# Separate written orders for the edge iterations of a software-pipelined Mamba and MoE layer

## What is computed

```python
q = rope(x @ W_in[:256].T);  h = rmsnorm(q)                       # part p
z, xBC, dt = split(h @ W_zxbcdt.T)                                # part a
xBC = silu(conv4(xBC));  dt = softplus(dt + dt_bias)
y = ssd(x_ssm, dt, A, B, C)           # chunked scan over the sequence, with a carried state
x1 = x + layernorm(q + rmsnorm(y * silu(z)) @ W_out.T)
w, idx = route(sigmoid(f @ router.T)) # f = layernorm(x1); 2 of 4 groups, 4 of 16 experts   # part f
acc = shared_ffn(f) + sum_e w_e * ffn_e(f)                        # silu(f @ G) * (f @ U) @ Wd
out = x1 + layernorm(acc)                                         # part g
```

## Time and profile before

| | us |
|---|---|
| median of 3 runs | 3214.55 (3213.54 to 3217.93) |
| the profiled execution | 3218.34 |
| its span, first to last instruction | 3216.4 |
| PE busy | 3116.9 (97%) |
| DVE, POOL, ACT busy | 2393.1, 2033.7, 1931.1 |
| PE's share of the chain that ended last | 94% |
| mean granted clock of PE | 0.991 |

### The profile page before, as it was taken

One profiled execution on the slowest core, in us unless ns is written; L12 is line 12 of the kernel. 1 busy time (PEld: TensorE's weight loads), 2 busy tenths in 40 slices (PEclk: granted clock), 3 DMA queues, 4 the chain that ended last, 5 costly groups with the idle time before them and its releaser, 6 DMA issues.

```text
span 3216.4 us, 62379 instructions
## 1 busy us (share of the span) xinstructions
PE 3116.9 (97%) x19648; PEld 2723.4 (85%) x19648; DVE 2393.1 (74%) x5104; ACT 1931.1 (60%) x4146; POOL 2033.7 (63%) x2311
## 2 busy tenths in 40 slices
PE   3699999999999999999999999999999999999997
PEld 3588888888888888888888888888888888888886
DVE  3777777777777777777777777777777777777772
ACT  3566665566665566665666665666665656665652
POOL 0466666766666776666776666776666776666764
PEclk9799999999999999999999999999999999999999
DMA  3122222222222222222222222222222222222221
GB/s 109 40 70 80 66 59 74 73 76 79 66 60 75 72 77 78 66 60 74 72 78 76 66 63 72 72 79 76 66 65 71 71 79 76 66 67 69 71 80 40
DMA packets 143434, 227.33 MB, mean 71 GB/s; under 512 B 18977, under 2 KB 88353, under 8 KB 143393
## 3 DMA queue, kind: packets, MB, share of 16 engines
q1 hardware_dynamic: 126496, 210.06, 19.9%
q0 software_dynamic: 16896, 16.78, 4.0%
HBM read 174.87 MB, written 35.13 MB: 65 GB/s over the span
## 4 chain that ended last, share of the span: by engine, by line
PE 94%; POOL 1%; DMA 0%; DVE 0%; ACT 0%; issue 0%; SPq 0%; POOLq 0%; ACTq 0%; DVEq 0%
PE fpb L1325 33%; PE apb L1325 19%; PE acc L1504 17%; PE apb L1450 7%; PE apb L1334 4%; PE ppb L1325 3%; PE apb L1435 3%; PE apb L1442 2%; PE ppb L1344 2%; PE apb L1422 1%; PE fpb L1374 1%; PE fpb L1344 1%; PE fpb L1376 1%; PE fpb L1483 0%; PE apb L1395 0%; POOL hid L541 0%
## 5 line engine op out<-in xcount | busy, mean ns | idle before, releaser
L546 POOL TENSOR_TENSOR hidL<-hid,hidH 128x512 fp32r<-128x512 f32 x384 | 545.8, 1421 | 216.8 <-ACT hidH L801 207.5
L1015 DVE SCALAR_TENSOR_TENSOR xc<-apb,cw,xc 128x511 f32<-128x511 f32 (+2 forms) x576 | 427.8, 748 | 67.8 <-ACT xc L714 39.5
L1504 PE MATMUL acc<-WDH,hidH 128*128 128x256 f32 x1536 | 458.2, 298 | 6.2 <-POOLq L548 5.9
L801 ACT CAST hidH<-hid 128x512 fp32r<-128x512 f32 x384 | 236.1, 615 | 353.6 <-POOL hid L541 288.7
L1504 PE MATMUL acc<-WDH,hidL 128*128 128x256 f32 x1536 | 432.0, 281 | 0.0
L1504 PE MATMUL acc<-WDL,hidH 128*128 128x256 f32 x1536 | 431.5, 281 | 0.0
L541 POOL TENSOR_TENSOR hid<-hid,cb 128x512 f32<-128x512 f32 x256 | 347.2, 1356 | 81.8 <-DVEq L1136 43.7
L1134 DVE TENSOR_TENSOR hid<-hid,fpb 128x512 f32<-128x512 f32 x384 | 261.1, 680 | 135.4 <-PE fpb L1325 125.2
L1325 PE MATMUL fpb<-fTh,UH 128*128 128x512 f32 x768 | 336.1, 438 | 0.8 <-ACTq L793 0.8
L732 ACT ACTIVATE seg<-seg,acs 128x128 f32<-128x128 f32 x1024 | 313.8, 389 | 10.2 <-ACT cb L782 5.9
L1325 PE MATMUL fpb<-fTh,GH 128*128 128x512 f32 x768 | 317.5, 413 | 0.0
(11 more groups left out here) (194 smaller groups left out, 8672.1 us busy)
## 6 DMA issues: line engine op xcount, KB each, us to landing
seg<-acs_row SPq DMA_DIRECT2D x128, 512.0 KB, 4.2
cb<-c_row SPq DMA_DIRECT2D x512, 128.0 KB, 2.9
xsP<-in_x SPq DMA_DIRECT2D x32, 512.0 KB, 3.6
xc<-qrot SPq DMA_DIRECT2D x32, 512.0 KB, 3.4
xc<-in_x SPq DMA_DIRECT2D x32, 512.0 KB, 4.3
out<-xc SPq DMA_DIRECT2D x32, 512.0 KB, 3.0
out<-xn POOLq DMA_DIRECT2D x32, 512.0 KB, 6.0
ZL_loaded<-in_wzx_t SPq DMA_DIRECT2D x2, 512.0 KB, 5.7
```

Of the source, the lines that this page charges most:

```text
L546: own.do(G.tensor_tensor(hidL[:, j % 2, :], hid[:, j % 2, :], hidH[:, j % 2, :].bitcast(fp32), ALU.subtract))
L801: A.copy(hidH[:, j % 2, :], hid[:, j % 2, :]).then_inc(sem["hidden_high"], 1)
L1015: ins = V.scalar_tensor_tensor(xc[:, b, s:], src[:, 0:T - s], cw[:, b, TAPS - 1 - s:TAPS - s], xc[:, b, s:], ALU.mult, ALU.add)
L1504: ins = nc.tensor.matmul(dst, l[:, w, tk], r[:, j, :], start=j == 0 and t % 2 == 0 and n == 0, stop=j == HB - 1 and n == 2, skip_group_che ...
```

## The change

Each engine's `iteration` with flags is replaced by six functions written out, `lead`, `first`, `iteration`, `tail`, `drain`, `last`. `iteration`, used for the second iteration (without g) and for the loop, emits what it did before. The other orders are new on all engines, and each has its own bank tables (`PLANS`, looked up by a small class `Way`), so that results of a part can go round the banks in another sequence. Counts per iteration are the same. The splits have a semaphore each (`s_high[n]`, `s_low[n]`) and are taken out of number order. The four constants that the lead needs are loaded apart, ahead of the others, with the semaphore `s_early`. The parts of the diff that set orders:

```diff
+        EARLY = ((ident[:], c_ident), (npwc[:], ...), (cos_t[:], ...), (sin_t[:], ...))
+        FIRST = ((cw[:], ...   # the other ten
...
@@ SP
             def load_consts():
+                load_split(0)
+                # EARLY on s_early; load_split(1); load_split(2); FIRST on s_const; load_split(3..11)
+            def first(i):
+                decay_store(); decay_rows(0); load_next(i + 1); decay_rows(1); decay_rows(2); decay_rows(3)
+                keep_q(); load_x(i)
@@ POOL
+            def lead():
+                norm_px(); rope_sum(0); root_q(0); rope_sum(1); root_q(1)
+            def first():
+                mask(0); decayed(0); mask(1); decayed(1); norm_px(); gated(0); mask(2); decayed(2); mask(3)
+                gated(1); gated(2); root_y(0); rope_sum(0); root_q(0); norm_mixed(0); gated(3); rope_sum(1)
+                root_q(1); root_y(1); norm_x1(0); norm_mixed(1); norm_x1(1)
+            def tail(i):
+                ... rest(9); norm_x1(0)
+                combine(10); norm_mixed(1); rest(10); combine(11); norm_x1(1); rest(11); result_stored()
+            def drain(i):
+                norm_out(); rest(0); add_result(i - 2); rest(1); rest(2); rest(3); hold_shift(); combine(4)
+                rest(4); combine(5); rest(5); ...; combine(10); rest(10); combine(11); rest(11)
@@ ACT
+            def lead():
+                norm_x(0); split_high(0); evac_xT(0); early_consts(); split_high(1); norm_x(1); split_high(2)
+                square_q(0); evac_xT(1); exp_table(); exp_a(); square_q(1); h_high(0); h_high(1)
+            def first():
+                split_high(9); silu_table(); silu_z(0, 0); split_high(4); silu_z(0, 1); silu_z(1, 0)
+                silu_z(2, 0); silu_z(1, 1); split_high(11); silu_z(3, 0); conv_first(4); exp_table()
+                softplus(); conv_first(5); silu_table(); conv_silu(4); conv_first(0); conv_silu(5)
+                conv_first(1); conv_silu(0); silu_z(2, 1); split_high(8); conv_silu(1); conv_first(2)
+                conv_first(3); silu_z(3, 1); split_high(3); conv_silu(2); conv_silu(3); exp_table(); decays()
+                evac_CB(); exp_seg(0); evac_B(); split_high(6); exp_seg(1); split_high(7); norm_x(0); norm_x(1)
+                exp_seg(2); evac_y(0); exp_seg(3); square_y(0); ...; norm_x1(0); norm_x1(1); silu_table()
+            def tail():
+                ... exp_seg(0); exp_seg(1); round_hidden(4); silu_table(); gate(5); gate(6); evac_y(0)
+                exp_table(); exp_seg(2); round_hidden(5); square_y(0); silu_table(); gate(7); exp_table()
+                exp_seg(3); evac_y(1); round_hidden(6); square_y(1); silu_table(); gate(8); round_hidden(7) ...
+                gate(10); gate(11); norm_x1(0); round_hidden(10); round_hidden(11); norm_x1(1)
@@ DVE
-            dve.wait_ge(s_const, 16 * len(FIRST))
+            def lead():
+                moments_px(); split_low(0); x_low(0); early_consts(); rope(0); x_low(1); norm_q(0); rope(1)
+                split_low(2); split_low(1); norm_q(1); h_low(0); h_low(1); negate_a()
+            def first():
+                dt_bias_add(0); split_low(9); dt_bias_add(1); dt_bias_add(2); dt_bias_add(3); split_low(4)
+                split_low(11); conv(4); conv(5); conv(0); dt_finish(); conv(1); evac_acs(); conv(2); conv(3)
+                split_low(3); split_low(8); times_dt(0); times_dt(1); decay_CB(0); moments_px(); new_state(0)
+                chunk_y(0); decay_CB(1); state_part(1); new_state(1); chunk_y(1); times_dt(2); state_part(2)
+                split_low(7); decay_CB(2); new_state(2); y_low(0); chunk_y(2); decay_CB(3); x_low(0); y_low(1)
+                times_dt(3); rope(0); mixed_out(0); state_part(3); split_low(10); y_low(2); x_low(1)
+                chunk_y(3); norm_q(0); rope(1); add_x(0); y_low(3); split_low(6); norm_q(1); h_low(0)
+                mixed_out(1); split_low(5); h_low(1); add_x(1)
+            def tail():
+                ... up(9); y_low(3); add_x(0); up(10); mixed_out(1); up(11); add_x(1)
+            def drain():
+                f_low(0); f_low(1); final_moments(); route_logits(); route_scores(); route_groups(); up(0)
+                up(1); route_experts(); up(2); up(3); ...; up(11)
@@ PE
-            pe.wait_ge(s_const, 16 * len(FIRST))
+            def lead():
+                early_consts(); x_by_channel(0); weights_split(0); project_q(0); x_by_channel(1); project_q(1)
+                h_by_channel(0); h_by_channel(1)
+            def first():
+                consts(); weights_split(1, 2); project_z(0, 0); project_z(0, 1); project_z(1, 0)
+                project_z(2, 0); project_z(1, 1); project_z(3, 0); project_x(4); project_x(5); project_x(0)
+                project_z(2, 1); project_x(1); cumulate(); project_x(2); project_x(3)
+                project_z(3, 1); x_by_token(0); CB(); x_by_token(1); B_by_token(); state(0); diagonal(0)
+                state(1); from_state(1); diagonal(1); x_by_token(2); from_state(2); state(2); ...
+                h_by_channel(1); weights_split(*range(4, len(SPLIT)))
+            def tail():
+                ... y_by_channel(3); down(8); up(10); project_out(3); gate(11); down(9); up(11)
+            def drain():
+                down(10); ffn_by_channel(0); ffn_by_channel(1); down(11); logits(0); logits(1)
+                gate(0); gate(1); up(0); up(1); gate(2); gate(3); down(0); up(2); down(1)
+                combine_by_expert(); gate(4); up(3); down(2); up(4); gate(5); down(3); up(5); gate(6); down(4)
+                up(6); gate(7); down(5); ...; up(9); gate(10); down(8); up(10); gate(11); down(9); up(11)
```

917 lines of the change are left out of this document (478 added, 439 removed).

## The result

The changed kernel took 3187.22 us, the median of four executions from 3186.01 to 3191.39. The kernel before took 3216.24 us beside it (four, from 3213.54 to 3220.29). The ratio is 0.9911, 95% interval 0.9894 to 0.9928: faster, by 29.0 us, which is more than the 0.2% that the prediction took as the limit. The profiled execution has a span of 3185.9 us against 3216.4 before, 30.5 less.

What follows compares the result with a forecast made beforehand. PE bounds the loop; only the edges, where PE mostly waits, were open. -18.5 - 11.7 + 0.5 + 1.0 - 5.8 = -34.5 us takes the profiled 3218.34 to 3183.8, as a median 3180.0; range 3169 to 3191.

Steps and rivals of the forecast that it cites:

- rival A: First iteration: hardly gets shorter, since another in-order wait replaces DVE's; -4 us there, 3188 us in all, chance 0.15.
- a loop pass that is not 96.0: Loop: each pass was to stay at 96.0 us; any other length would make the prediction wrong.
- Lead, -18.5 forecast: Lead: moments first and only four early constants let norm_x(0) start at 8.4 instead of 27.27 us; -18.5 us.
- cover 3.61 us, need 3.03: nothing: Lead: DVE's two splits, 3.03 us, fit its 3.61 us between rope(1) and norm_q(1) and cost nothing.
- First iteration, -4.8 - 6.9 forecast: First iteration: DVE's wait before conv(3) goes, -4.8; splits moved into DVE's waits, -6.9; bounds -4 and -23 us.
- Rival B: First iteration and drain: denser order keeps PE at the higher clock level; first -20, drain -7.5, 3170 us, chance 0.12.
- C: Whole kernel: only the lead's -18.5 us come and the orders bring nothing; 3196 us, chance 0.06.
- Second iteration, +0.5 forecast: Second iteration: the second half of the FFN input comes about 4.4 us in instead of 1.8; +0.5 us (0 to +3).
- Tail, +1.0 forecast: Tail: DVE takes up(11) before add_x(1), so the logits start at about 100.8 us against 99.76; +1.0 (-1 to +5).
- Rival D: Tail: a second 1.28 us behind each of ten table loads could put 5 us on PE; 3185 us, chance 0.04.
- Rival E: Tail: gate waits behind exp_seg in ACT's one queue, so PE loses ACT's busy time; 3221 us, slower, chance 0.02.
- Drain, -5.8 forecast: Drain: c_ready about 14 us after the logits, no PE wait from down(4) to up(11), faster end; 62.9 to 57.1 us.

## Why the prediction was right, and what its sum missed

The forecast was 3180.0 us, the measurement 3187.22, inside the range of 3169 to 3191; faster was given 0.96. For the profiled execution the sum said 3183.8, and it took 3187.6: these 3.8 us are those of the table. The other 3.4 us come from turning it into a median. The sum took off 3.8 us, since the profiled execution before lay that far above the median of three; the profiled execution of the changed kernel lies only 0.4 above its own median. By the number alone the median is nearer to rival A's 3188 than to the forecast; that the forecast's mechanism held, and not A's, is read from the stretches. In its first paragraph the prediction also has 311.8 us for the four open stretches, which add up to 310.8, and 2784 us for the loop, which takes 2795.5; neither enters the sum. Its sign of being wrong "a loop pass that is not 96.0" was set on a window and not on a pass: the pass is 96.4 us before and after.

1. **Lead, -18.5 forecast, -17.9 measured.** The chain from moments to `norm_x` (3.87 us forecast; 4.51 to 8.39, 3.88 us) and the nothing for constants and `split_high` were right. The term that was wrong is "cover 3.61 us, need 3.03: nothing". The cover was there; what cost was `rope_sum(1)` being held up by the splits, 1.25 us on the chain. The prediction had named GpSimd stretching VectorE's operation and not the other way round, and it is the other way round that lies on the chain.
2. **First iteration, -4.8 - 6.9 forecast; -3.2 and -7.5 measured in the profile after.** `times_dt(0)` came at 31.5 us instead of 29.9. In five further runs with that order and a granted clock of 0.84 to 0.93 ahead of it, it came at 29.2 to 30.0, and in two at 0.71 at 31.9, against 34.67 before and 34.5 in the run with the lead alone: the order does give the 4.8 us. The sum took the clock of one execution before (0.85 there) for granted; in the profile after it was 0.77. The step is right, its size hangs on the level. The other part, from 61.56 us down to 54.04, and to 50.6 in the run with the old drain (clock 0.86), was sized a little low. Of the time of the splits behind `times_dt(0)` somewhat more than half counts, as the run without four of them shows; the bounds -4 and -23 were not touched.
3. **Rival B** (TensorE stays at the higher level) did not come by itself: 0.78 against 0.79. But its mechanism is real: with extra matmuls the clock went to 0.96 and the first iteration to 76.7 us, -19.6, near the -20 that the rival had. It was the right lever with nothing in the change to pull it. Rival A (the first iteration hardly shorter) is excluded by its stretch, -10.7 us, and A and C (only the lead works) by the run with the lead alone: 3200.72 against 3187.22. In the two profiles the first two iterations have 7.2 us of that difference, tail and drain 3.2.
4. **Second iteration, +0.5 forecast, +1.3 measured.** Forecast was that the FFN's input comes later. It did; what was missed is a table load of 1.28 us right behind `norm_x1(1)` on ACT, in front of `conv_first(4)`. With that load and the split moved the stretch took 97.2 us in two profiles, and 97.8 and 98.8 in the two with extra matmuls besides. In others with the change's orders it took 98.1 to 99.96 us, and 102.2 behind the 98 extra matmuls; what makes the difference was not followed.
5. **Tail, +1.0 forecast, +2.2 measured.** The order of events was as walked, the sizes were not: `add_x(1)` took 1.92 us instead of 0.88, beside `combine(11)`. In the changed kernel's second profile it took 0.88 us, the wait was 2.52 and the tail 100.6, +0.8: the forecast's +1.0 is the order, and the rest is that collision, which comes in some executions:

```profile
3107.33 0.88 DVE L1219 SCALAR_TENSOR_TENSOR xc<-xc,rstd 128x256 f32<-128x256 f32 x2 [0.24 <-DVE hid L1249]
```

Rival D (dearer table loads) left no trace: each of the ten loads took 1.28 us, and in nine cases the next operation came 0.01 to 0.02 us behind; in the tenth ACT waited 1.12 us for GpSimd's mask. Rival E (an ACT queue too full) neither.
6. **Drain, -5.8 forecast, -5.5 measured,** and the run with the old drain gives 5.8 for it. The walk was right step by step.

## What to carry to other kernels

A schedule that is written out by hand hides work well in one engine's waits, but what it costs is set by what runs beside it: put a long VectorE operation, above all one with two SBUF sources, where GpSimd has nothing on the chain, not merely where VectorE is idle. Where an edge of the kernel alternates between short work and waits on TensorE, look at the granted clock as well as at the order: 225 matmuls whose results nobody reads were worth 4.8 us, beside 10.7 us for all that the change did to the first iteration; and the drain's order with the logits first, in which TensorE fell to the lower level each time, cost some 5 us. And take more than one profile before a difference of a few microseconds in one stretch is explained.

## What the runs showed of the hardware

- The same 298 matmuls of the first iteration, same order, were granted 0.74 to 0.86 of the clock in different executions, and the stretch took 85.5 to 80.4 us. The single executions of the changed kernel spread over 5 us. In the three kernels with TensorE kept busy in the lead and the first iteration they spread over 3.4, 2.3 and 6.5, so that a smaller spread is not shown.
- In the tail TensorE kept the higher level through waits of 1.12 and 3.75 us in one profile and lost it for part of a stretch (0.79 from 3102 to 3110 us) after the same two in another; it kept it through 1.30 and 2.52 us and lost it after 1.31 and 2.52. In the four profiles with the logits ahead of `down(11)` it always went, after waits of 4.27 us in two of them, 2.48 and 1.99 in one, 0.58 and 2.01 in one, and tail and drain together took some 5 us more. What decides between two executions with the same waits stays open. The Trainium skill (TensorE: Matmul & The Clock Gate, HAM oscillation) warns that waits between bursts bring the lower level back; the trace agrees in that the level never fell there without a wait before it.
- A GpSimd operation on two values for each partition took 1.60 us instead of 0.19 beside a split of 1.72 us on VectorE, and in the drain an operation of VectorE on 64 values took 2.58 us instead of 0.23, while GpSimd issued the store of the output (1.36 us) and did a `rest` (1.80). In proportion the smallest operations were stretched the most, and here they stood on chains.
